# Batch tiles paired with a shift, and every stage placed by a position on one axis

## The chip, the cores and the metric

The kernel runs on one core of a Trainium2 chip. The metric is the device time of one execution in microseconds (us). The core has TensorE (PE) for matmuls, VectorE (DVE), ScalarE (ACT) and GpSimd (POOL); SyncE (SP), ACT and POOL also issue transfers. All data is float32, so each matmul of the program shows as two records in the trace.

## The reference

1024 users are in the batch, each with 50 rows of 300 numbers (`x`) and 200 label rows of 300 numbers. K = 200 labels, E = 300.

```python
mask = sign(sum(abs(x), axis=2))
q1 = attn_pool(x, mask, w1, b1, w2)          # softmax over the 50 rows of exp of a score, then a weighted sum
q2 = attn_pool(x, mask, w3, b3, w4)
h = concatenate([q1, q2], axis=1) @ w5 + b5  # 1024 x 300
f6 = h @ w6 + b6
iu, ju = triu_indices(300, k=1)              # 44850 pairs
g = (v @ v.T)[iu, ju]
cross = h[:, iu] * h[:, ju] * g              # 1024 x 44850
f7 = cross @ w7 + b7                         # w7: 44850 x 300
out8 = concatenate([f6, f7], axis=1) @ w8 + b8
return einsum('bu,bku->bk', out8, label_embedding)
```

## The kernel before

**Tiles and units.** The 1024 users are eight batch tiles of 128. The 44850 pairs are laid out as 351 tiles of 128 pairs (`NT`), grouped in 91 units (`NU`) of mostly four tiles. A unit's left factors are one 128-row tile of h (transposed, pairs on the partitions), its right factors a buffer `sring` that is read back from a copy of h in DRAM (`hrows`); 25 such buffers (`BUFS`) serve the 91 units, three are resident at a time (`SSLOTS`). The last three units ("own") take both factors from such buffers, 26 small transfers for six buffers.

**Main stage.** Two batch tiles form a group (`GB = 2`, `L = 256` columns), and four groups follow one another, 91 units each. For each unit DVE makes the products (`products`, L867: left x right over n x 256 columns into `cring`, four slots, so DVE may be four units ahead of PE). PE multiplies each product tile with its w7 tile (`unit`, L546): n x 2 matmuls of 128 x 128 by 128 x 300 into one PSUM bank for each batch tile. w7 is read once per group: ACT issues a load for every two units (`w7_load`, up to 8 tiles, 1200 KB) two blocks ahead into `wring` (three slots) and multiplies each w7 tile by its factor g (`w7_scale`, L695) two units ahead.

**Pooling.** The batch is 16 halves of 64 users. For one half DVE makes 56 score rows (`score_row`, L795, 128 x 300 each), ACT 28 absolute sums (`absolute`, L627), then come small steps: `exps`, `maxima`, `softexp`, `weights` (L834), 28 narrow matmuls (`pool_rows`, L496), `denominators`, a transpose (`turn`, L484) and, for several halves together, the product with w5 (`mix`, 18 matmuls, L511), which gives h. `features_out` writes it to `hT` and to DRAM. x comes in pieces of 128 x 7 x 300 (1050 KB, L336), four for a half, through nine slots.

**Labels.** `label_row` (L893) multiplies a label row of 128 users with `out8` and sums over 300: 200 rows for each batch tile. SP loads them in chunks of five rows (750 KB, L340) through 13 slots, in the memory that x used. After the main stage four of every five chunks are shared: DVE makes the product of the whole chunk (L889), ACT the five sums (`sums`, L704).

**Order.** Every engine's program is written out over phases: phase -1 is the head (halves 0 to 3, before the first unit), phases 0 to 3 are the four groups, phase 4 is the tail (80 chunks of labels, the last two batch tiles). The other twelve halves all lie in units 0 to 74 of phase 0 (`HALVES`, `X_UNTIL = 75`), the labels of group g in units 11 to 90 of the phase after it. In the head `fold_w8` stands at step 9. Three units before the end of each group `out8_from_f6` puts eight matmuls (four for each batch tile) on PE. All engines run their lists in order.

## Time and profile before

| | |
|---|---|
| runs of the kernel before | 1917.06 us median of 3 (1915.41 to 1917.81) |
| the profiled execution | 1916.95 us, its span 1915.2 us |
| first main matmul (L546) | 169.44 us |
| last main matmul ends | 1759.8 us |
| PE, DVE, ACT busy | 1626.4, 1437.1, 1014.9 us |
| moved | 590.69 MB, mean 308 GB/s |

The span runs from the first to the last instruction of the profiled execution; the execution's time is 1.75 us more. The table cuts it in three: a head up to the first main matmul, the main stage, and a tail of labels. In a row with a start, the first number is the start and the second the duration, both in us.

### The profile page before, as it was taken

The page shows a single profiled execution, that of the slowest core. Times are in us where ns is not written, and L with a number is a line of the kernel's source. Part 1 is how long each engine was busy: PE and PEld are TensorE (multiplying, and loading weights), DVE is VectorE, ACT ScalarE, POOL GpSimd, SP SyncE. Part 2 cuts the span into 40 slices and gives each one's busy share as a digit, 9 for nine tenths or more (in the row PEclk, how much of TensorE's full clock was granted, in tenths as well). Part 3 has the DMA queues.
Part 4 walks back from the last instruction along what each step waited for, and adds up shares of the span by engine and source line. Part 5 has one row for each costly group of instructions (what it writes and reads, how often), then busy time and mean ns, then how long its engine had stood idle before and what let it go on. Part 6 is the DMA issues. An engine that isn't in the chain of part 4 may idle for free.

```text
span 1915.2 us, 24356 instructions
## 1 busy us (share of the span) xinstructions
PE 1626.4 (85%) x7106; PEld 1173.8 (61%) x7106; DVE 1437.1 (75%) x5126; ACT 1014.9 (53%) x3118; POOL 41.3 (2%) x86
## 2 busy tenths in 40 slices
PE   0656899998999999999999999999999999998000
PEld 0334666666667677777776777777677777775000
DVE  8764999899893257778763777787447777874996
ACT  4434677677674344444444444444344444543998
POOL 0001000100100100000000000000000000000000
PEclk9757999999999999999999999999999999999555
DMA  6247567566665979999997899999979999997996
GB/s 271 107 164 263 209 245 291 220 261 260 229 229 202 348 290 357 364 367 368 413 343 268 312 362 361 361 389 407 291 261 364 357 364 357 404 390 221 401 417 247
DMA packets 112003, 590.69 MB, mean 308 GB/s; under 512 B 13940, under 2 KB 29069, under 8 KB 81661
## 3 DMA queue, kind: packets, MB, share of 16 engines
q1 hardware_dynamic: 81373, 368.22, 51.5%
q10 hardware_dynamic: 27680, 217.89, 29.4%
q0 software_dynamic: 2816, 3.01, 0.5%
q8 instruction: 57, 0.93, 0.2%
q14 instruction: 77, 0.63, 0.1%
HBM read 585.28 MB, written 3.79 MB: 308 GB/s over the span
## 4 chain that ended last, share of the span: by engine, by line
PE 67%; DVE 17%; ACT 9%; issue 3%; DMA 3%; POOL 0%; SPq 0%; ACTq 0%; DVEq 0%; POOLq 0%
PE bank L546 60%; DVE junk L795 11%; ACT stream L704 7%; PE bank L511 3%; DVE cring L867 3%; PE bank L496 2%; DMA sring<-hrows 2%; ACT absjunk L627 1%; DVE wts L834 1%; PE bank L559 1%; DMA wring<-in_w7p 1%; PE bank L554 0%; DVE small L824 0%; DVE small L823 0%; PE bank L484 0%
## 5 line engine op out<-in xcount | busy, mean ns | idle before, releaser
L546 PE MATMUL bank<-wring,cring 128*128 128x300 f32 x5616 | 1442.0, 419 | 50.8 <-DVE cring L867 50.0
L546 PEld LDWEIGHTS bank<-wring,cring 128*128 128x128 f32 x5616 | 1067.5, 191 | 417.8 <-DVE cring L867 63.3
L695 ACT ACTIVATE wring<-wring,gcol 128x300 f32<-128x300 f32 x1404 | 636.1, 532 | 674.6 <-DMA wring<-in_w7p 469.7
L893 DVE SCALAR_TENSOR_TENSOR stream<-stream,out 128x300 f32<-128x300 f32 x1280 | 519.5, 464 | 0.0
L867 DVE TENSOR_TENSOR cring<-lefts,sring 128x1024 f32<-128x1024 f32 (+2 forms) x232 | 274.7, 1186 | 178.1 <-PE bank L546 173.7
L795 DVE SCALAR_TENSOR_TENSOR junk<-stream,ubc 128x300 bf16<-128x300 f32 x896 | 356.8, 463 | 0.0
L867 DVE TENSOR_TENSOR cring<-hT,sring 128x1024 f32<-128x1024 f32 (+1 forms) x120 | 144.5, 1206 | 146.3 <-PE bank L546 125.8
L627 ACT ACTIVATE absjunk<-stream 128x300 bf16<-128x300 f32 x448 | 195.6, 439 | 0.5
L704 ACT ACTIVATE stream<-stream 128x300 f32<-128x300 f32 x320 | 139.4, 449 | 0.0
L496 PE MATMUL bank<-stream,wts 128*32 128x300 f32 x896 | 68.2, 461 | 52.4 <-DVE small L837 52.4
L889 DVE TENSOR_TENSOR stream<-stream,out 128x1500 f32<-128x1500 f32 x64 | 105.8, 1712 | 4.9 <-ACT out L614 4.9
L893 DVE DVE_READ_ACCUMULATOR stream<-stream,out 128x1 f32 x1280 | 103.5, 81 | 0.0
L627 ACT ACTIVATION_READ_ACCUMULATOR absjunk<-stream 128x1 f32 x448 | 84.6, 189 | 0.0
L496 PEld LDWEIGHTS bank<-stream,wts 128*32 128x32 f32 x896 | 30.6, 120 | 87.6 <-issue 62.4
L795 DVE DVE_READ_ACCUMULATOR junk<-stream,ubc 128x1 f32 x896 | 71.6, 80 | 0.0
L867 DVE TENSOR_TENSOR cring<-sring 128x1024 f32<-128x1024 f32 (+1 forms) x12 | 11.5, 955 | 72.4 <-issue 43.5
L511 PE MATMUL bank<-poolT,w5sb 128*128 128x64 f32 (+7 forms) x252 | 62.3, 392 | 4.0 <-ACT poolT L614 4.0
L704 ACT ACTIVATION_READ_ACCUMULATOR stream<-stream 128x1 f32 x320 | 63.7, 199 | 0.0
L511 PEld LDWEIGHTS bank<-poolT,w5sb 128*128 128x128 f32 (+3 forms) x252 | 41.9, 217 | 24.8 <-issue 12.2
L617 ACT ACTIVATE hT<-bank,bcol 128x64 f32<-128x64 f32 (+3 forms) x21 | 8.0, 381 | 66.2 <-PE bank L511 66.2
L834 DVE TENSOR_TENSOR wts<-small,onehot 128x896 f32<-128x896 f32 x16 | 17.4, 1086 | 23.5 <-ACT small L640 23.5
L484 PE MATMUL bank<-ident,flat 128*128 128x128 f32 (+1 forms) x72 | 13.1, 303 | 25.7 <-ACT flat L644 24.9
(59 smaller groups left out, 220.8 us busy)
## 6 DMA issues: line engine op xcount, KB each, us to landing
stream<-in_label SPq DMA_DIRECT2D x320, 750.0 KB, 8.7
wring<-in_w7p ACTq DMA_DIRECT2D x164, 1200.0 KB, 8.5
stream<-in_x SPq DMA_DIRECT2D x64, 1050.0 KB, 9.4
sring<-hrows SPq DMA_DIRECT2D x76, 512.0 KB
wring<-in_w7p ACTq DMA_DIRECT2D x8, 1050.0 KB, 7.7
wring<-in_w7p ACTq DMA_DIRECT2D x8, 600.0 KB, 6.7
sring<-hrows SPq DMA_DIRECT2D x16, 176.0 KB
lefts<-hrows SPq DMA_DIRECT2D x20, 128.0 KB, 3.3
```

What stands on the lines that cost most here:

```text
L496: pe.matmul(dst[j * M:(j + 1) * M, 0:E], wts[:, j * T + t].rearrange("p h b -> p (h b)"), xring[:, (s * XCH + c) % XSLOTS, t - CHUNK[c][1] ...
L511: mm = pe.matmul(dst[0:n, 0:nb], w5sb[0:nk, q, o:o + n], poolT[0:nk, q % NCH, q // NCH, b0:b0 + nb], start=(q == 0), stop=(q == 2 * NCH - 1))
L546: mm = pe.matmul(acc[(g * GB + b) % 4][:, 0:E], lhs, w, start=(t == 0), stop=(t == NT - 1))
L559: mm = pe.matmul(dst[:, 0:E], f7T[0:n, b, c, :], w8sb[0:n, NCH + c, :], start=False, stop=(c == NCH - 1))
L627: nc.scalar.activation(absjunk[:, k % 2, :], xring[:, n % XSLOTS, t - CHUNK[c][1], :], ACT.Abs, accum_out=absum[:, s % 3, at:at + 1]).then ...
L695: ins = nc.scalar.activation(w, w, ACT.Copy, scale=gcol[:, t:t + 1])
L704: ins = nc.scalar.activation(row, row, ACT.Copy, accum_out=score[:, m % GB, q0 + k:q0 + k + 1])
L795: ins = nc.vector.scalar_tensor_tensor(out=junk[:, k % 2, r % 2, :], in0=xring[:, n % XSLOTS, t - CHUNK[c][1], :], scalar=1.0, in1=ubc[:, ...
L834: nc.vector.tensor_tensor(wts[:], prob[k].rearrange("p h t -> p t h").unsqueeze(3).to_broadcast([P, TT, 2, UB]), onehot[:].unsqueeze(1).un ...
L867: nc.vector.tensor_tensor(cut(cring[:, k % CSLOTS]), in0, cut(sring[:, nb % SSLOTS]), ALU.mult).then_inc(c_ready, 1)
L889: nc.vector.tensor_tensor(rows, rows, out8[:, m % (2 * GB), :].unsqueeze(1).to_broadcast([P, LR, E]), ALU.mult).then_inc(l_product, 1)
L893: ins = nc.vector.scalar_tensor_tensor(out=row_in, in0=row_in, scalar=1.0, in1=out8[:, m % (2 * GB), :], op0=ALU.mult, op1=ALU.mult, accum ...
```

## The change

The phases go; every stage has a position on one axis instead, from -34 (`START`) to 473. Positions 0 to 406 (`POS = 407`) are units of the main stage; unit p uses the unit table at p mod 91.

- **Pairs with a shift.** Even batch tiles begin at positions 0, 91, 182, 273, odd ones at 43, 134, 225, 316 (`SHIFT = 43`), each for 91 positions; an odd tile begins in the middle of the table and wraps around. So positions 0 to 42 have one batch tile, 43 to 363 two, 364 to 406 one. In numbers of the table: 167 tiles with one matmul each, 1237 with two, 167 with one; 2808 matmuls in all, as before.
- **Single units.** Where one batch tile is live, DVE makes the products with one `scalar_tensor_tensor` of 128 columns for each tile, which takes in the factor g, and w7 isn't scaled by ACT; PE waits for the w7 load itself. Where two are live, product and scaling are as before, with 4-dimensional operands.
- **w7** is streamed in rounds of 91 positions: 206 blocks, where it was 184.
- **h in DRAM** is kept for each batch tile by itself (`hrows[b]`, rows of 128 numbers, where they were 256), so a buffer of two live tiles is two loads. Left tiles lie in `lefts` for four batch tiles. POOL stores repeated rows with fewer transfers (`again`).
- **Pooling** of the halves goes by the list `DOTS`: halves 0 and 1 in positions -34 to -21, half 2 in -20 to -7, half 3 in -6 to 5, halves 4 and 5 to 42, 6 to 9 in 43 to 88, and 10 to 15 in stretches of 14 positions every 23, to 228. `mix` follows for each batch tile (seven of the eight behind position 0). From half 10 on x has four slots, one half.
- **Labels** begin at position 102 (`LATER = 11` behind a tile's end). Batch tiles 0 to 5 have theirs over the 43 or 48 positions that follow, at half the rate inside `DOTS`; 65 rows of tile 6 lie in 375 to 406. 67 chunks are left for the tail, where there were 80. The label ring has 7 slots until x is done and 13 then.
- **out8** is made for each batch tile in one piece (`out8_all`) four positions behind its end; `out8_from_f6` ahead of the group's end is gone.
- `fold_w8` and `folded_out` stand at -23 (step 11), and the first two w7 loads behind them.

```diff
-    GB = 2
-    G = NBT // GB
-    L = GB * P
+    SHIFT = next(k for k, u in enumerate(UNITS) if u[1] == 6)
+    BEGIN = [NU * (b // 2) + SHIFT * (b % 2) for b in range(NBT)]
+    END = [p + NU for p in BEGIN]
+    POS = END[-1]
...
+    DOTS = [(-34, -27), (-27, -20), (-20, -6), (-6, 6), (6, 24), (24, 43), (43, 54), (54, 65), (65, 77), (77, 89),
+            (100, 114), (123, 137), (146, 160), (169, 183), (192, 206), (215, 229)]
...
+    WIDE = 10
+    X_SLOT = [n % XSLOTS if n < WIDE * PARTS else XSLOTS - PARTS + n % PARTS for n in range(NS * PARTS)]
...
+    EXP, MAX, SOFT, WEIGH, POOL, DEN, POOL_OUT, TURN, MIX = range(9)
+    LATE = (0, 1, 1, 2, 3, 8, 8, 9, 12)
+    HEAD = {0: (0, 2, 3, 3, 3, 6, 7, 7, 0), 1: (0, 1, 1, 2, 2, 6, 6, 6, 7)}
+    X_FREE = 7
...
+    NARROW = LSLOTS - 6
...
             def s_load(n):
-                g, buf = n // BUFS, n % BUFS
...
+                for b in live_at(n):
+                    tiles = sring[:, n % SSLOTS, b % 2]
...
+                    if buf < OWN:
...
+                        sp.dma_start(tiles.rearrange("p j l -> p (j l)"), src).then_inc(s, 16)
+                        continue
...
+            for q in range(START, STOP):
+                for n in [n for n in range(XSLOTS, NS * PARTS) if DOTS[X_BEFORE[n] // PARTS][1] + X_FREE == q]:
+                    x_load(n)
...
+            def unit(p):
...
+                pe.wait_ge(c_ready, p + 1)
+                if SHIFT <= p < SHIFT + BOTH:
+                    pe.wait_ge(w7_ready, p - SHIFT + 1)
+                else:
+                    pe.wait_ge(w7_in[n_block % WSLOTS], 16 * (n_block // WSLOTS + 1))
...
+                    for b in live(p):
+                        mm = pe.matmul(acc[b % 4][:, 0:E], cring[0:rows, p % CSLOTS, b % 2, j0 + j, :], w,
+                                       start=(p == BEGIN[b] and j == 0), stop=(p == END[b] - 1 and j == n - 1))
...
+            def products(p):
...
+                if len(tiles) == 1:
+
+                    b = tiles[0]
+                    for j in range(j0, j0 + n):
...
+                        ins = nc.vector.scalar_tensor_tensor(
+                            out=cring[0:rows, p % CSLOTS, b % 2, j, :], in0=one, scalar=gcol[0:rows, t:t + 1],
+                            in1=sring[0:rows, nb % SSLOTS, b % 2, j, :], op0=ALU.mult, op1=ALU.mult)
+                    ins.then_inc(c_ready, 1)
+                    return
...
```

## Rows read from the trace of the kernel before

**Rows 1.** The page: busy time of each engine, and TensorE's clock in 40 slices.

```profile
PE 1626.4 (85%) x7106; PEld 1173.8 (61%) x7106; DVE 1437.1 (75%) x5126; ACT 1014.9 (53%) x3118; POOL 41.3 (2%) x86
...
PEclk9757999999999999999999999999999999999555
```

**Rows 2.** Windows: stretch, length, busy us (records) of PE, PEld, DVE, ACT, POOL, PEclk, DMA share, GB/s.

```profile
170.00:300.00 130.00, 116.16 (x588) 80.83 (x587) 128.07 (x556) 96.33 (x341) 0.00 (x0) 0.98 0.66 246
800.00:990.00 190.00, 190.00 (x754) 142.94 (x753) 151.62 (x532) 84.11 (x187) 0.56 (x1) 1.00 0.98 378
990.00:1034.00 44.00, 41.46 (x154) 28.83 (x153) 17.59 (x50) 13.47 (x30) 0.55 (x1) 0.96 0.87 280
1766.00:1915.00 149.00, 0.00 (x0) 0.00 (x0) 134.24 (x224) 139.59 (x641) 1.08 (x2) 0.51 0.86 347
```

**Rows 3.** Groups by line and shape: busy us, mean ns | idle before, releasers.

```profile
L546 PE MATMUL bank<-wring,cring 128*128 128x300 f32 x5600 | 1437.4, 419 | 50.8 <-DVE cring L867 50.0 <-ACT wring L695 0.6
...
L893 DVE SCALAR_TENSOR_TENSOR stream<-stream,out 128x300 f32<-128x300 f32 x1280 | 519.5, 464 | 0.0
L795 DVE SCALAR_TENSOR_TENSOR junk<-stream,ubc 128x300 bf16<-128x300 f32 x896 | 356.8, 463 | 0.0
...
L867 DVE TENSOR_TENSOR cring<-lefts,sring 128x256 f32<-128x256 f32 x8 | 3.4, 425 | 16.0 <-PE bank L546 11.6 <-DMA lefts<-hrows 4.4
```

**Rows 4.** Timeline of DVE in phase 0: start, duration, instruction.

```profile
186.07 1.22 DVE L867 TENSOR_TENSOR cring<-lefts,sring 128x1024 f32<-128x1024 f32 x1
187.21 0.46 DVE L795 SCALAR_TENSOR_TENSOR junk<-stream,ubc 128x300 bf16<-128x300 f32 x1
...
187.60 0.46 DVE L795 SCALAR_TENSOR_TENSOR junk<-stream,ubc 128x300 bf16<-128x300 f32 x1
...
204.72 0.17 DVE L814 TENSOR_SCALAR masked<-absum 128x28 f32<-128x28 f32 x1
...
206.96 1.22 DVE L867 TENSOR_TENSOR cring<-hT,sring 128x1024 f32<-128x1024 f32 x1
```

**Rows 5.** Chain of waits in the head, 33 to 90 us: start, duration, what.

```profile
47.33 6.47 PE bank L496 x54
...
61.76 0.41 ACT brow L614
...
72.21 8.63 PE bank L511 x36
```

**Rows 6.** Timeline of PE at the first main matmul.

```profile
169.44 10.13 PE L546 MATMUL bank<-wring,cring 128*128 128x300 f32 x32 [12.61 <-DVE cring L867]
```

**Rows 7.** Transfers issued from 300 to 430 us: count, KB each, median us to landing.

```profile
wring<-in_w7p ACTq DMA_DIRECT2D x12, 1200.0 KB, 5.7
```

**Rows 8.** Transfers issued from 800 to 990 us.

```profile
stream<-in_label SPq DMA_DIRECT2D x49, 750.0 KB, 8.1
wring<-in_w7p ACTq DMA_DIRECT2D x22, 1200.0 KB, 8.8
```

**Rows 9.** Chain of waits, the whole span: PE's side work.

```profile
312.74 3.66 PE bank L496 x54
...
498.91 9.66 PE bank L511 x36
...
1041.59 3.62 PE bank L559 x12
```

**Rows 10.** Timeline of all engines at the end of phase 1.

```profile
1001.02 1.22 DVE L867 TENSOR_TENSOR cring<-sring 128x1024 f32<-128x1024 f32 x1 [7.38 <-DMA sring<-hrows]
...
1002.27 1.14 SPq L382 DMA_DIRECT2D sring<-hrows  x3
...
1017.03 1.22 DVE L867 TENSOR_TENSOR cring<-sring 128x1024 f32<-128x1024 f32 x1 [12.83 <-issue]
...
1018.31 15.48 PE L546 MATMUL bank<-wring,cring 128*128 128x300 f32 x52 [2.54 <-DVE cring L867]
```

**Rows 11.** Timeline of PE at the last main matmuls.

```profile
1754.30 5.51 PE L546 MATMUL bank<-wring,cring 128*128 128x300 f32 x20
```

More of the change, by code:

```diff
@@ L139, in rec_kernel @@
     LSLOTS = 13
+    ROUNDS = [1 << k for k in range(FOLD.bit_length() - 1)]
     SSLOTS = 3
@@ new lines, in rec_kernel @@
+    LATER = 11
+    EARLY_ROWS = 65
+    LABELS_BY = {START - 1: 0}
+    for q in range(START, POS):
+        done = 0
+        for b in range(NBT - 1):
+            steps = range(END[b] + LATER, END[b + 1] + LATER if b < NBT - 2 else POS)
+            share = [1 if any(a <= k < z for a, z in DOTS) else 2 for k in steps]
+            rows = K if b < NBT - 2 else EARLY_ROWS
+            done += rows * sum(w for k, w in zip(steps, share) if k <= q) // sum(share)
+        LABELS_BY[q] = done
+    TAIL_CHUNKS = (NBT * K - LABELS_BY[POS - 1]) // LR
@@ L152, in rec_kernel, with labels_by, released @@
+    def labels_by(q):
+        return LABELS_BY[min(q, STOP - 1)]
+    def released(n):
+        return (l_summed if SHARED[n] else l_used), sum(SHARED[k] == SHARED[n] for k in range(n + 1))
     ctx = ExitStack()
```

687 lines of the change are left out of this document (328 added, 359 removed).

## The prediction

> **What bounds the kernel now.** I read the busy shares first. PE is busy 85% of the span and DVE 75%, so neither binds throughout, and the last three slices have PE's clock at half: that is the tail, which has no matmuls [rows 1]. So the span is read in three parts, and each part has its own limit.
>
> The head lasts 169.4 us until the first main matmul, which came after DVE's first product [rows 6]. Four halves are pooled one behind another there.
>
> The main stage lasts 1590.4 us, to 1754.30 + 5.51 = 1759.8 [rows 11]. In its steady phases PE is busy 190 of 190 us, 754 records, 0.252 us each, so 0.504 us for one matmul of the program [rows 2]; 2808 of them are 1415 us. PE stood 50.8 us ahead of these matmuls, nearly all for DVE's products [rows 3]. DMA is at a share of 0.98 and 378 GB/s in the same window, so I take 385 GB/s as the most that this mix of transfers gets. In phase 0 it is DVE that is full: 128.07 of 130 us, PE 116.16 [rows 2]. There a position costs nine score rows at 187.60 - 187.21 = 0.39 us and a product of 1.14 us (186.07 to 187.21), 4.66 in all [rows 4], against eight matmuls, 4.03. A half adds 2.24 us of small steps (204.72 to 206.96) and about 1.5 for weights and denominators. Over 75 positions and twelve halves DVE needs some 395 us, PE 350 to 360.
>
> The tail lasts 1915.2 - 1759.8 = 155.4 us. ACT is busy 139.59 of 149 there, DVE 134.24 [rows 2]: 64 shared chunks on ACT, 2.18 us each; what is left, 9.6 us behind ACT's last sum, is the last store and the end.
>
> **Part 1, the head: 169.4 becomes 110.** Two halves instead of four must be pooled for the first product, but 196 score rows stand ahead of it in DVE's list. These are 77 us from about 12. ACT is held by `folded_out` until 61.76 + 0.41 [rows 5], as before; then eight absolute sums at 0.44, and `maxima` of half 1 starts near 67, weights end near 72, `pool_rows` at the low clock takes up to 6.5 us [rows 5], the mix of tile 0 ends near 90 (8 to 9 us [rows 5]). ACT waits for this mix and then has 14 absolute sums of half 2, to 97; DVE's `maxima` of half 2 waits for them, and about 19 score rows and the weights follow: the first single product near 109.5. The loads of h end before (first A store near 88, left tiles by 106). I take 110, bounds 104 and 118.
>
> **Part 2, positions 0 to 42, one tile: 116.** PE: 167 matmuls x 0.504 = 84, two `pool_rows` at 3.66 [rows 9], three transposes, one mix of 128 columns, a slow start of the clock: 102. DVE: 140 score rows (55 us), small steps 8, and 167 products of 128 columns. This instruction isn't in the trace. From below, 128 columns at the pace of a 1024-column product (1.14 for 1024) are 0.14; from above, a 256-column product lasts 0.425 [rows 3] and half of its columns are 0.13 less, 0.29. Score and label rows of 300 columns last 0.46 [rows 3] and issue every 0.39; the 1024-column product less the 256-column one is 0.80 us for 768 columns, 0.13 for 128, and 0.07 of its 1.14 is left over for the start: 0.20. I take 0.20: 33 us, DVE 96, bounds 88 and 111. DMA: w7 is needed at full rate for half the work, 25 MB, and twelve x pieces fall in here (13 MB), h 2.7 MB: 41 MB, 106 us at 385 GB/s. It doesn't come evenly. A w7 block is 4.03 us of PE work here (1.23 MB, 305 GB/s). It landed in 5.7 us where SP's queue had gaps [rows 7] and in 8.8 where labels filled it [rows 8]. 1.23 MB at 385 GB/s are 3.2 us, which leaves 2.5 for the way; 8.8 less 2.5 is 195 GB/s, half. So while four x pieces drain, w7 gets 190 GB/s, 6.4 us for a block, and 22 us of this lose 8 us each time. Three bursts, the first while three blocks are resident, PE's side work covering some: 14 us on top of 102. Bounds 102 and 130.
>
> **Part 3, positions 43 to 363, two tiles: 1409.** PE: 2474 matmuls, 1247 us; eleven `pool_rows` 40; transposes 5; six mixes, whose group form took 9.66 [rows 9], taken at 6.5, 39; six `out8_all` and transposes at 5 (half of [rows 9]'s 3.62, and four matmuls of f6 more), 30: 1361. Short dips of the clock add 5: one is in the window of 990 to 1034, 0.96 [rows 2]. DVE: 347 us of products, 560 score rows, 1154 label rows, eleven times small steps, some 1060: hidden in sum, and in the densest stretch (positions 100 to 236: 936 rows, 147 us of products, 22 us of steps, 536 of PE's 597) too. Phase 0's loss goes away, since its score rows are spread over 229 positions.
>
> Two waits take a part back. First, the own units. Buffer 22 can load only behind product 88. Before, it was issued at 1002.27 and product 89 came at 1017.03; PE stood 2.54 us [rows 10], with the 5.3 us of `out8_from_f6` in between. That cover is gone, and the buffer is six transfers on SP's queue and not three, buffer 23 ten and not five, with rows half as long. So 8 + 4 us where labels share the queue; three such places in here and at 364, less where the queue is less full: 25 (bounds 5 and 45). Second, SP's queue in positions 100 to 236. The stretch moves 91 MB of labels, 21 of x, 82 of w7 and 19 of h, 213 MB in 597 us, 357 GB/s of 385. x has one half's slots, so the four pieces are issued two positions (8 us) before the first is read, behind label loads. DVE would stand about 12 us for each of six halves; it is up to four units, 16 us, ahead of PE, and has about 10 us to spare in each 23 positions. I take 3 us a half, 18 (bounds 0 and 70). Sum 1361 + 5 + 25 + 18.
>
> One rule of the Trainium skill bears on the rate. Its page "DMA: Bandwidth & Descriptors", section Bandwidth, gives about 358 GB/s as what one core gets from HBM; the window at 378 GB/s [rows 2] is above it, so the measurement stands. By 358 the two single stretches would be 114 and 119 us.
>
> **Part 4, positions 364 to 406, one tile: 113.** PE has 84 + 5, DVE 43 + 33. DMA has 23 MB of w7, 23 label chunks (17.7 MB) and 2 MB of h: 42.7 MB, 111 us. In the first eleven positions labels come at 4.2 rows a position, and w7 gets its half: 35 us where PE needs 22. The rest, 28 MB, is 73 us. With some start 113; bounds 92 and 130.
>
> **Part 5, the tail: 129.** 67 chunks, 53 shared: 53 x 2.18 = 115.6 us on ACT, DVE 115. Three to four us for tile 7's f7 and out8, then the 9.6 as before. Labels of tile 6 are there at once, so the 4 us start on `out` goes. Bounds 125 and 134.
>
> **Sum:** 110 + 116 + 1409 + 113 + 129 = 1877 us of span, plus 1.75: **1879 us**, against 1916.95 of the same profiled execution and 1917.06 of the median. Against before: head -59, main stage +48, tail -26. 0.2% (3.8 us) is about what a measurement of this kernel can tell.
>
> **Rivals.**
> - *A, the likeliest (0.50):* as above; its own range is 1850 to 1910.
> - *B, PE bounds it all (0.23):* w7 is favoured or buffered enough in the single stretches, and the own loads hide. Then 106 + 103 + 1375 + 94 + 127 + 2 = 1807, up to 1850. For it: DMA at 0.98 and PE at 190 of 190 in one window [rows 2]. Against it: there PE asked for 152 GB/s of w7, not 305.
> - *C, SP's queue starves DVE, slower (0.17):* the 12 us of waiting for x in each of six halves come through whole, because a wait of DVE also delays its products and its lead isn't won back in the score stretch (4.3 us a position on DVE, 4.03 on PE). Then 54 us more than in A, 1933. It decides from 34 us more, 6 us a half. For it: 357 of 385 GB/s, one queue in order. Against: 16 us of lead.
> - *D, the clock falls in the single stretches (0.05):* gaps in PE's work at w7 waits could drop it to 1.2 GHz, a matmul to 1.01 us. Each single stretch that ran so throughout would last 169 + side work, 60 us more: 1939 for one. Against it: 0.98 with PE at 116 of 130 us [rows 2]. For it: the clock's low level in the head, where PE is busy in pieces [rows 1]. The Trainium skill, "TensorE: Matmul & The Clock Gate", section HAM oscillation, tells of such a kernel, whose waits for DMA brought the clock down in every round; this rule is what D is.
> - *E, gains and losses cancel (0.05):* 1913 to 1921.
>
> **Chances.** A gives 0.49 faster and 0.01 same; B 0.23 faster; C 0.14 slower, 0.02 same, 0.01 faster; D 0.04 slower, 0.01 faster; E 0.02 same, 0.02 slower, 0.01 faster. Together: faster 0.75, same 0.05, slower 0.20. The range for 8 in 10 cuts off the lower half of B and the upper half of C and D: 1825 to 1932.
>
> **What the profile will show.** First main matmul at 104 to 118. In positions 0 to 42 and 364 to 406 PE idle until w7 lands, DMA share over 0.95 and w7 landing in 8 us or more; B if PE is over 95% busy there. DVE's label and score rows waiting for `in_x` and `in_label` in 500 to 900 us: a few us a half for A, over 10 for C. Single products 0.20 us apart. PE waiting for `cring` some 10 us at positions 89 to 91 of each round. The clock's line below 9 in the single stretches would be D. The prediction is wrong if label loads keep w7 out longer than half, or if a wait of ACT in its new order (a mix, x) holds back the scaling of w7, which I costed at nothing because it is two units ahead.

## The result, and the profile after

The changed kernel takes 1860.16 us (median of 4 runs, 1856.23 to 1862.87); the kernel before took 1916.93 (4 runs). The ratio is 0.9709, with a 95% interval of 0.9695 to 0.9724: faster by 2.9%. The forecast was 1879 us, in a range of 1825 to 1932, so the time is 19 us under it and inside case A's own range. The profiled execution took 1859.29 us, its span is 1857.5.

The first main matmul of a position cuts the span in stages:

| stage (positions) | forecast, us | after, us | before, us |
|---|---|---|---|
| head | 110 | 106.7 | 169.4 |
| 0 to 42, one tile | 116 | 118.8 | |
| 43 to 363, two tiles | 1409 | 1397.6 | |
| 364 to 406, one tile | 113 | 105.1 | |
| main stage together | 1638 | 1621.5 | 1590.4 |
| tail | 129 | 129.2 | 155.4 |
| span | 1877 | 1857.5 | 1915.2 |

So the head gives 62.7 us, the tail 26, and the main stage takes back 31. The page of the kernel after, to be held against [rows 1]: busy times, and TensorE's clock.

```profile
PE 1615.5 (87%) x7142; PEld 1165.1 (63%) x7142; DVE 1479.9 (80%) x5516; ACT 919.1 (49%) x2844; POOL 33.4 (2%) x62
...
PEclk9889999999999999998999999999999999999655
```

PE is busy 11 us less than before in a span that is 58 shorter. The windows of the four stages behind the head, columns as in [rows 2]:

```profile
106.70:225.50 118.80, 102.88 (x507) 71.42 (x508) 108.17 (x500) 38.12 (x157) 3.52 (x6) 1.00 0.87 340
225.50:1623.10 1397.60, 1373.77 (x6004) 1008.01 (x6002) 1074.40 (x3973) 708.89 (x1918) 23.95 (x41) 0.99 0.89 332
1623.10:1728.20 105.10, 93.98 (x351) 64.23 (x351) 95.11 (x400) 1.71 (x5) 0.54 (x1) 1.00 1.01 418
1728.20:1857.50 129.30, 9.13 (x18) 4.12 (x17) 109.75 (x181) 117.15 (x535) 1.08 (x2) 0.51 0.81 326
```

In both single stretches PE has idle time: 15.9 us in the first, 11.1 in the second. The second has the DMA engines at a share of 1.01; the first has DVE busy 108 of 119. With two tiles PE is busy 98% of the time. What PE waited for in the first, by the view of waits (us in total, times, longest; 2.1 us of the first line lie ahead of the first main matmul):

```profile
PE bank L600 <- DVE cring L905: 10.9, 10, 2.2
...
PE bank L600 <- DMA wring<-in_w7p: 7.1, 5, 2.1
```

In the second it is 8.6 us for w7 and 2.9 for products. The groups that answer to [rows 3], and two more (L905 is the product of a single unit, L917 that of a pair, L935 the label row, L819 the score row):

```profile
L600 PE MATMUL bank<-wring,cring 128*128 128x300 f32 (+1 forms) x5616 | 1448.0, 419 | 52.8 <-DVE cring L917 19.6
...
L935 DVE SCALAR_TENSOR_TENSOR stream<-stream,out 128x300 f32<-128x300 f32 x1335 | 546.4, 466 | 0.9 <-DMA stream<-in_label 0.2
L917 DVE TENSOR_TENSOR cring<-lefts,sring 128x1024 f32<-128x1024 f32 (+2 forms) x309 | 368.3, 1193 | 205.1 <-PE bank L600 202.6
L819 DVE SCALAR_TENSOR_TENSOR junk<-stream,ubc 128x300 bf16<-128x300 f32 x896 | 364.2, 466 | 4.3 <-DMA stream<-in_x 4.2
...
L905 DVE SCALAR_TENSOR_TENSOR cring<-lefts,gcol,sring 128x128 f32<-128x128 f32 x334 | 95.2, 348 | 16.8 <-PE bank L600 15.7
...
L917 DVE TENSOR_TENSOR cring<-sring 128x1024 f32<-128x1024 f32 (+1 forms) x12 | 11.5, 956 | 72.4 <-DMA sring<-hrows 49.1
```

Three readings come from here. Score rows waited 4.2 us for x in all, label rows 0.2 for labels: SP's queue starved nobody. The products of the own units (the last group, twelve of them) waited 72 us on DVE, most of it for `sring`; this is a wait of DVE, of which PE sees what is left when its four units of lead are used up. And PE's idle time ahead of the main matmuls is 52.8 us where it was 50.8 [rows 3]. But 12.6 of the 50.8 lay ahead of the very first main matmul [rows 6], in the head, and only 2.1 of the 52.8 do. Inside the main stage PE's idle time has grown, and it lies elsewhere: 15.7 us of it are waits for w7 itself, 19.6 are waits for products of pairs, nearly all at the own units.

### The profile page after: what moved, and what is told of

It is laid out like the page before. It is cut to its first block, busy times and chain, and to the rows that moved or that the text cites. A ratio compares the mean times of both kernels' runs of the same rounds, so it can differ in the third digit from the quotient of the medians.

```text
span 1857.5 us, 25035 instructions
## 1 busy us (share of the span) xinstructions
PE 1615.5 (87%) x7142; PEld 1165.1 (63%) x7142; DVE 1479.9 (80%) x5516; ACT 919.1 (49%) x2844; POOL 33.4 (2%) x62
## 3 DMA queue, kind: packets, MB, share of 16 engines
q1 hardware_dynamic: 105157, 368.23, 52.8%
## 4 chain that ended last, share of the span: by engine, by line
PE 72%; DMA 7%; ACT 7%; DVE 7%; SPq 4%; issue 2%; ACTq 0%; POOL 0%; DVEq 0%; POOLq 0%
PE bank L600 64%; ACT stream L747 6%; DMA wring<-in_w7p 5%; DVE junk L819 3%; PE bank L549 3%; SPq L438 3%; PE bank L563 2%; DMA sring<-hrows 2%; DVE stream L935 1%; PE bank L612 1%; PE bank L610 1%; DVE cring L917 1%; DVE cring L905 1%; ACT absjunk L663 1%; SPq L444 0%
## 5 line engine op out<-in xcount | busy, mean ns | idle before, releaser
L600 PE MATMUL bank<-wring,cring 128*128 128x300 f32 (+1 forms) x5616 | 1448.0, 419 | 52.8 <-DVE cring L917 19.6
L600 PEld LDWEIGHTS bank<-wring,cring 128*128 128x128 f32 (+1 forms) x5616 | 1064.1, 191 | 420.8 <-DVE cring L905 30.4
L738 ACT ACTIVATE wring<-wring,gcol 128x300 f32<-128x300 f32 x1237 | 565.1, 533 | 608.8 <-PE bank L600 340.3
L935 DVE SCALAR_TENSOR_TENSOR stream<-stream,out 128x300 f32<-128x300 f32 x1335 | 546.4, 466 | 0.9 <-DMA stream<-in_label 0.2
L917 DVE TENSOR_TENSOR cring<-lefts,sring 128x1024 f32<-128x1024 f32 (+2 forms) x309 | 368.3, 1193 | 205.1 <-PE bank L600 202.6
L819 DVE SCALAR_TENSOR_TENSOR junk<-stream,ubc 128x300 bf16<-128x300 f32 x896 | 364.2, 466 | 4.3 <-DMA stream<-in_x 4.2
L747 ACT ACTIVATE stream<-stream 128x300 f32<-128x300 f32 x265 | 115.5, 441 | 0.1
L935 DVE DVE_READ_ACCUMULATOR stream<-stream,out 128x1 f32 x1335 | 109.9, 82 | 0.0
L905 DVE SCALAR_TENSOR_TENSOR cring<-lefts,gcol,sring 128x128 f32<-128x128 f32 x334 | 95.2, 348 | 16.8 <-PE bank L600 15.7
L931 DVE TENSOR_TENSOR stream<-stream,out 128x1500 f32<-128x1500 f32 x53 | 89.6, 1717 | 3.5 <-DMA stream<-in_label 1.8
L819 DVE DVE_READ_ACCUMULATOR junk<-stream,ubc 128x1 f32 x896 | 74.0, 83 | 0.0
L917 DVE TENSOR_TENSOR cring<-sring 128x1024 f32<-128x1024 f32 (+1 forms) x12 | 11.5, 956 | 72.4 <-DMA sring<-hrows 49.1
L747 ACT ACTIVATION_READ_ACCUMULATOR stream<-stream 128x1 f32 x265 | 50.5, 190 | 0.0
L563 PE MATMUL bank<-poolT,w5sb 128*128 128x128 f32 (+3 forms) x288 | 48.2, 297 | 1.0 <-ACT poolT L652 0.8
L563 PEld LDWEIGHTS bank<-poolT,w5sb 128*128 128x128 f32 (+3 forms) x288 | 35.2, 164 | 14.4 <-issue 4.5
L655 ACT ACTIVATE lefts<-bank,bcol 128x128 f32<-128x128 f32 x16 | 5.9, 366 | 43.6 <-PE bank L563 42.7
## 6 DMA issues: line engine op xcount, KB each, us to landing
stream<-in_x SPq DMA_DIRECT2D x64, 1050.0 KB, 12.6
```

The lines of the kernel that those rows point to most:

```text
L563: mm = pe.matmul(dst[0:n, 0:P], w5sb[0:nk, q, o:o + n], poolT[0:nk, q % NCH, q // NCH, :], start=(q == 0), stop=(q == 2 * NCH - 1))
L600: mm = pe.matmul(acc[b % 4][:, 0:E], cring[0:rows, p % CSLOTS, b % 2, j0 + j, :], w, start=(p == BEGIN[b] and j == 0), stop=(p == END[b] - ...
L738: ins = nc.scalar.activation(w, w, ACT.Copy, scale=gcol[:, t:t + 1])
L747: ins = nc.scalar.activation(row, row, ACT.Copy, accum_out=score[:, m % 2, q0 + k:q0 + k + 1])
L819: ins = nc.vector.scalar_tensor_tensor(out=junk[:, k % 2, r % 2, :], in0=xring[:, X_SLOT[n], t, :], scalar=1.0, in1=ubc[:, hd, 0:E], op0=A ...
L905: ins = nc.vector.scalar_tensor_tensor(out=cring[0:rows, p % CSLOTS, b % 2, j, :], in0=one, scalar=gcol[0:rows, t:t + 1], in1=sring[0:rows ...
```

## The experiments

Each kernel is the changed one with the edit shown. Stage times are read as in the table above.

**Half of w7 in the single stretches.** Each block of positions 0 to 42 and 364 to 406 loads its first half alone and uses it twice, which leaves out half of those blocks' w7.

```diff
+                z = a + half(n) * E
                 act.dma_start(wring[:, n % WSLOTS, 0:z - a], w7p[:, a:z]).then_inc(w7_in[n % WSLOTS], 16)
```

> The changed kernel, but in positions 0 to 41 and 364 to 406 each w7 block loads only half of its tiles (the second half of the tiles is multiplied with the first half's weights, so half of w7 is left out there). If DMA bounds the single stretches (my theory): the first goes from 118.8 us to 104 to 108, the second from 105.1 to 92 to 95, the run 20 to 25 us shorter. If DVE bounds them (busy 108 of 118.8 and 95 of 105.1 us): no more than 3 us each.

Measured: 1840.27 us, ratio 0.9606 (0.9586 to 0.9626). The first stretch took 112.5 us (-6.3), the second 94.0 (-11.1), the rest is within 2 us. So the forecast of this experiment held in the second stretch and was too high in the first (104 to 108 were expected). The windows of both stretches:

```profile
106.80:219.30 112.50, 102.35 (x507) 71.59 (x508) 107.76 (x499) 38.66 (x159) 3.52 (x6) 1.00 0.72 261
1619.10:1713.00 93.90, 91.80 (x352) 65.86 (x351) 92.58 (x395) 2.00 (x7) 0.54 (x1) 0.98 0.92 335
```

With DMA no longer full, PE is busy 91.80 of 93.90 us in the second: transfers were its bound. In the first PE still idles 10 us, and DVE is busy 107.76 of 112.50.

**One wide product in the single stretches.** The factor g is left out there, so that DVE makes one product of all tiles of a unit.

```diff
-                    for j in range(j0, j0 + n):
...
-                        ins = nc.vector.scalar_tensor_tensor(
...
+                    nc.vector.tensor_tensor(cring[0:rows, p % CSLOTS, b % 2, j0:j0 + n, :],
+                                            left_of(left, b)[0:rows].unsqueeze(1).to_broadcast([rows, n, P]),
```

> The changed kernel, but where one batch tile is live the product of a unit is one tensor_tensor over all its tiles without the factor g (g is left out there). It should last 0.6 us where four single ones take 1.05, 19 us less of DVE in each single stretch. If DVE bounds them: 118.8 us becomes 105 to 109 and 105.1 becomes 95 to 98, the run 15 to 22 us shorter. If DMA bounds them: no more than 3 us each.

Measured: 1853.11 us, ratio 0.9674 (0.9658 to 0.9690). The first stretch took 115.0 us (-3.8), the second 105.2, unchanged. The interval lies just beside that of the changed kernel. **Both edits together**:

> e1_half_w7 and e2_wide together (half of w7 and the factor g left out in the single stretches). Alone they took 6.3 and 3.8 us off the first single stretch of 118.8 us. If DMA and DVE take turns there, and the one hides what the other frees: 102 to 107. If something else holds it (PE's side work, ACT): 108 to 112.

One run, 1828.85 us. The first stretch took 107.6 us (-11.2, against 6.3 and 3.8 alone), the second 91.2 (-13.9). With one run of it, a difference of 1 us isn't read. So the first stretch is held by transfers and by DVE in turns, the second by transfers, with DVE next behind them.

**w7 scaled by ACT in the last stretch.** This puts the factor g back to ACT from position 43 on, so DVE makes wide products in the last stretch and the result is the full one.

```diff
-                if SHIFT <= p < SHIFT + BOTH:
+                if SHIFT <= p:
...
-                    if SHIFT <= q + AHEAD < SHIFT + BOTH:
+                    if SHIFT <= q + AHEAD < POS:
```

> The changed kernel, but in positions 364 to 406 ACT, which is idle there (1.7 of 105 us busy), scales w7 two units ahead as in the paired stretch, and DVE makes one product for a unit. DVE has 19 us less. If DMA bounds this stretch: 105.1 us stays or becomes up to 110, since w7 is wanted two units earlier. If DVE's products do: 95 to 98.

Measured: 1871.19 us, ratio 0.9766 (0.9740 to 0.9792), slower than the changed kernel. The last stretch took 117.5 us, 12.4 more. DVE had been no bound there. The waits of this kernel say what took its place: ACT waited 36.2 us for w7 loads in the stretch, and PE 11.7 us for ACT's scaling. A w7 block is needed two units earlier, and the transfers were full already. About half of the 12.4 us is TensorE's clock: in the window of 1623 to 1740 us its mean is 0.94, PE is busy 99.8 us where it was 94.0 in the changed kernel, and from 1636 to 1644 the granted clock is 0.50 with PE at work, after a stretch of 8 us in which PE was busy 4.8.

**Plain loads for the own units.** Every own buffer is loaded like any other, as one transfer of 128 rows of 2 KB for each tile; the pairs of these units are then wrong ones.

```diff
-                    if buf < OWN:
+                    if buf < BUFS:
...
-                return len(live_at(n)) * (1 if buf < OWN else (5, 5, 3, 3, 5, 5)[buf - OWN])
+                return len(live_at(n)) * 1
```

> The changed kernel, but the six buffers of the own units are each loaded by one plain transfer for a batch tile, where they take 26 (the pairs of these units are wrong, their number of bytes is higher). If the number of transfers on SP's queue is what delays them: PE's gaps at positions 89 to 91 (0.8, 10, 2.7, 3.7 us by round) go below 2 us and positions 176 to 186 from 61.2 us to 40 to 45, the run 12 to 25 us shorter. If it is the label loads queued ahead of them: within 5 us of the changed kernel.

Measured: 1838.09 us, ratio 0.9603 (0.9581 to 0.9624). The pair stretch took 1375.5 us, 22.1 less, the others within 2.3 us of the changed kernel. The own units come four times; the time of the positions around each, in us, with the kernels of the next three experiments:

| positions | changed | plain loads | issued by ACT | in one transfer | left once |
|---|---|---|---|---|---|
| 85 to 94 | 45.6 | 41.9 | 45.5 | 41.9 | 42.4 |
| 176 to 185 | 61.2 | 49.0 | 50.1 | 59.0 | 58.3 |
| 267 to 276 | 40.4 | 39.7 | 51.9 | 50.0 | 39.0 |
| 358 to 369 | 44.5 | 38.3 | 48.7 | 48.0 | 40.8 |

Each column is one profiled execution. How far such a number can be trusted is told by the kernels whose own loads are the changed kernel's (half of w7, wide product, both, scaled by ACT, and `fold_w8` first, further down): they have 43.3 to 45.7 us at the first place, 59.3 to 61.8 at the second, 40.2 to 46.2 at the third and 40.3 to 48.7 at the fourth, which runs into the last stretch, where most of them differ. So a difference of a few us at one place says little, and the 40.4 of the changed kernel at the third is on the low side. Their pair stretches took 1392.0 to 1401.6 us.

Here is the second of these places in the changed kernel, all engines (L438, L444 and L446 are the small transfers on SP's queue):

```profile
828.01 1.23 DVE L917 TENSOR_TENSOR cring<-sring 128x1024 f32<-128x1024 f32 x1 [9.41 <-DMA sring<-hrows]
...
829.26 7.32 SPq L438 DMA_DIRECT2D sring<-hrows  x6
...
836.75 1.29 SPq L444 DMA_DIRECT2D sring<-hrows  x4
...
840.20 0.29 SPq L446 DMA_DIRECT2D sring<-hrows  x1
...
842.04 1.23 DVE L917 TENSOR_TENSOR cring<-sring 128x1024 f32<-128x1024 f32 x1 [10.07 <-issue]
```

And PE there:

```profile
843.32 7.43 PE L600 MATMUL bank<-wring,cring 128*128 128x300 f32 x20 [8.60 <-DVE cring L917]
```

Product 88 waits 9.4 us for its buffers, and only when it is done may SP load the last buffer of product 89 (number 22), six transfers that take 7.3 us to issue; product 89 comes 14 us after product 88, and PE stands 8.6 us.

The first of the four places is the comparison that matters most. The transfers are the same, six for buffer 22 among them, but no label is loaded yet:

```profile
428.40 1.23 DVE L917 TENSOR_TENSOR cring<-sring 128x1024 f32<-128x1024 f32 x1 [8.69 <-DMA sring<-hrows]
...
434.16 1.22 DVE L917 TENSOR_TENSOR cring<-sring 128x1024 f32<-128x1024 f32 x1 [2.57 <-issue]
```

Product 89 comes 5.8 us after product 88 there. In the three later rounds, with label loads in SP's queue, it comes 14.0, 13.2 and 17.2 us after it. With plain loads the four distances are 6.6, 6.7, 8.1 and 7.3 us. So small transfers are not late by themselves; they are late in the rounds that load labels, and there plain ones hardly are. The windows of 820 to 860 us, the changed kernel:

```profile
820.00:860.00 40.00, 29.47 (x107) 20.89 (x106) 19.66 (x87) 14.32 (x45) 0.00 (x0) 0.87 0.77 233
```

and with plain loads:

```profile
820.00:860.00 40.00, 36.01 (x159) 24.96 (x161) 32.22 (x134) 20.98 (x60) 0.00 (x0) 0.91 0.93 350
```

While the small transfers run, all transfers together bring 233 GB/s with the engines at a share of 0.77; with plain ones they bring 350 at 0.93. Three further kernels vary how the small transfers are issued.

**The own loads issued by ACT** instead of SP. ACT issues a load three places earlier in its list than SP did, behind a wait for the same product of DVE.

```diff
+                    if t == q + 3 and n + SSLOTS in BUFFERS and (n + SSLOTS) % BUFS >= OWN:
+                        act.wait_ge(c_ready, t + 1)
+                        loads[0](n + SSLOTS, act)
```

> The changed kernel with the loads of the own units' six buffers issued by ACT (which waits for DVE's product three positions ahead of its own place) and not by SP. Theory (they wait in SP's list and behind its label loads): PE's gaps at positions 88 to 91 (10 and 3.7 us in the second and fourth round) go below 3 us, positions 176 to 186 from 61.2 us to 45 to 52, the run 8 to 20 us shorter. Rival (the transfers themselves, their number and half-length rows, are the time, in whatever queue; or ACT, held by its wait, is late with the scaling of w7): within 5 us of the changed kernel, or slower.

Measured: 1875.32 us, ratio 0.9785 (0.9759 to 0.9812), 15 us slower than the changed kernel. The second place took 50.1 us for 61.2, inside what was expected of it: product 89 comes 8.4 us after product 88 there, not 14.0, with the same six transfers.

```profile
832.39 1.22 DVE L926 TENSOR_TENSOR cring<-sring 128x1024 f32<-128x1024 f32 x1 [10.49 <-issue]
...
840.75 1.23 DVE L926 TENSOR_TENSOR cring<-sring 128x1024 f32<-128x1024 f32 x1 [4.39 <-issue]
```

The gap of 8.6 us is gone, but PE has new ones, of 6.6 us at this place, 4.7 at the third, and 5.3 and 3.6 at the fourth. All but the last end with ACT's scaling of w7: ACT is late for it, since its own list stands while it waits for DVE and issues. The waits of this kernel in the pair stretch, two rows of them (what waited, for what: us in total, times, longest):

```profile
ACT wring L742 <- issue: 47.6, 8, 7.2
...
PE bank L604 <- ACT wring L742: 20.8, 12, 6.6
```

**Both tiles' rows in one transfer** where the shape allows it. The rows of all tiles lie in one tensor; the number of issues falls, bytes and row length stay. The ordinary buffers become one transfer for both tiles too. The transfers over 44, 44 and 40 partitions stay one for each tile, so buffer 22, for which product 89 waits, has six transfers as before.

```diff
-        hrows = [nc.dram_tensor(f"hrows{b}", [A_ROWS + B_ROWS + C_ROWS + D_ROWS, P], F32, kind="Internal").ap()
-                 for b in range(NBT)]
+        hall = nc.dram_tensor("hall", [NBT * RB, P], F32, kind="Internal").ap()
...
+                    src = bass.AP(hall.tensor, (BASE[b0] + row) * P, [[rpitch, r1 - r0], [step, nt], [1, P]])
+                    sp.dma_start(dst, src).then_inc(s, 16)
```

> The changed kernel with the DRAM copies of h in one tensor, so that a buffer of two live batch tiles is one transfer (the own units' six buffers 38 a round and not 52, buffers 23 and 24 five each and not ten). The bytes and the lengths of rows are unchanged. Theory (the number of transfers that SP must issue): PE's gaps at positions 88 to 91 shrink, positions 176 to 186 from 61.2 us to 50 to 56, the run 6 to 15 us shorter. Rival (e3_own_plain gained by other things: longer rows, no spread over few partitions): within 3 us of the changed kernel.

Measured: 1869.63 us, ratio 0.9771 (0.9742 to 0.9800), slower than the changed kernel. PE's longest gaps at the last three places are 10.1, 7.8 and 8.4 us where they were 8.6, 1.5 and 3.7. Since buffer 22 is loaded as before (product 89 comes 14.4 us after product 88 at the second place), this kernel doesn't tell whether fewer issues for it would help; its loss lies elsewhere and isn't traced. The window shows that merging the others didn't make the transfers faster as a whole:

```profile
820.00:860.00 40.00, 29.26 (x104) 20.08 (x102) 21.42 (x95) 14.26 (x44) 0.00 (x0) 0.87 0.82 247
```

**Left buffers of the own units loaded once over 128 rows.** Their three transfers of 44, 44 and 40 rows read the same repeated rows, so one transfer of 128 brings the same data.

```diff
-                        for k, (r0, r1) in enumerate(((0, REST), (REST, 2 * REST), (2 * REST, P))):
+                        for k, (r0, r1) in enumerate(((0, P),) if left else ((0, REST), (REST, 2 * REST), (2 * REST, P))):
```

> The changed kernel with the left factors of the first two own units (buffers 20 and 22) read in one transfer over 128 partitions for each batch tile, not three over 44, 44 and 40 (the repeated rows in DRAM hold the same numbers, so the result is the same): 44 transfers a round and not 52, and buffer 22, which can only be asked for behind product 88, is two transfers and not six. Theory (a transfer over few partitions in short rows is slow on DMA, and buffer 22 is the one that DVE stands for): product 89 comes 3 to 6 us earlier behind product 88 in positions 88 to 91, positions 176 to 186 from 61.2 us to 52 to 57, the run 5 to 12 us shorter than the changed kernel, the fastest version so far. Rival (as in e9_merged, the buffers behind it hold DVE just as long): within 4 us of the changed kernel.

Measured: 1847.51 us (6 runs, 1845.52 to 1852.04), ratio 0.9637 (0.9609 to 0.9664). This is the fastest version that computes the whole reference; its interval doesn't meet that of the changed kernel, and it is some 0.7% under it. The pair stretch is 1384.7 us, 12.9 less, and under all those of 1392.0 to 1401.6. The same place in this kernel:

```profile
822.48 1.22 DVE L917 TENSOR_TENSOR cring<-sring 128x1024 f32<-128x1024 f32 x1 [7.45 <-DMA sring<-hrows]
...
823.73 1.97 SPq L438 DMA_DIRECT2D sring<-hrows  x2
...
835.67 1.22 DVE L917 TENSOR_TENSOR cring<-sring 128x1024 f32<-128x1024 f32 x1 [9.22 <-issue]
...
836.94 7.43 PE L600 MATMUL bank<-wring,cring 128*128 128x300 f32 x20 [5.79 <-DVE cring L917]
```

Two transfers are issued in 1.97 us where six took 7.32, and yet product 89 comes 13.2 us after product 88 and not 14.0. So the time of issuing is not what it waits for; the landing is. Bytes and row length are those of the changed kernel, so the gain comes with fewer and wider transfers alone. The 12.9 us come in pieces of 1 to 4 at the four places, each too small to be told from the spread above; only their sum can.

What holds the landing stays open between two causes. In both kernels SP issued a label load of 750 KB shortly ahead of buffer 22 (at 826.78, 2.5 us ahead, in the changed kernel), and the first round, which has none, is quick. And a w7 load on ACT's queue was under way: from 836 to 838 us it brought 0.45 MB while all of SP's queue brought 0.04; in the first round w7 loads were issued at 424.5 and 433.0 us, and none between the two products. No run takes one of them away and leaves the rest.

**No shift.** `SHIFT = 0`: tiles run in pairs as before, all stages by positions, halves 0 to 3 in the head, the other twelve in positions 0 to 228; labels over the 91 positions behind a pair.

```diff
-    SHIFT = next(k for k, u in enumerate(UNITS) if u[1] == 6)
+    SHIFT = 0
...
-    DOTS = [(-34, -27), (-27, -20), (-20, -6), (-6, 6), (6, 24), (24, 43), (43, 54), (54, 65), (65, 77), (77, 89),
+    DOTS = [(-36, -29), (-29, -22), (-22, -15), (-15, -8), (0, 17), (17, 34), (34, 51), (51, 67), (67, 78), (78, 89),
```

> The changed kernel with SHIFT = 0: two batch tiles begin together as before the change, four halves are pooled in the head, 364 positions, 80 chunks of labels in the tail; score rows spread over the positions, storage of h by batch tile and all else as in the changed kernel (out8 of the odd tile six positions later). If the shift is what gains: head 150 to 160 us, main stage 1550 to 1575, tail 152 to 158, 1870 to 1895 in all, 10 to 35 us slower than the changed kernel. If the spreading of the score rows is the gain and the shift only pays its own costs: 1865 or less.

Measured: 1917.50 us (10 runs), ratio 0.9996 (0.9983 to 1.0010): no difference from the kernel before, and slower than either expectation. The head took 153.1 us, the four rounds 395.4, 410.7, 418.3 and 373.5, the tail 166.2. The tail is long because labels were held back four positions and the odd tile's `out8` six, which this edit needed. Windows of the four rounds, first the kernel before:

```profile
169.40:654.70 485.30, 452.88 (x2332) 311.64 (x2332) 405.11 (x1689) 325.07 (x1110) 27.09 (x54) 0.99 0.66 243
654.70:1025.40 370.70, 367.28 (x1439) 272.32 (x1438) 263.17 (x890) 160.88 (x362) 1.11 (x2) 1.00 0.94 353
1025.40:1394.60 369.20, 366.55 (x1439) 272.55 (x1438) 263.55 (x892) 160.91 (x362) 1.08 (x2) 1.00 0.93 349
1394.60:1759.80 365.20, 365.14 (x1439) 271.49 (x1438) 261.95 (x890) 158.88 (x357) 0.68 (x2) 1.00 0.93 348
```

and this one:

```profile
153.10:548.50 395.40, 390.62 (x1811) 287.50 (x1811) 256.64 (x887) 239.10 (x722) 7.02 (x12) 0.99 0.62 223
548.50:959.20 410.70, 398.45 (x1778) 291.40 (x1779) 332.06 (x1272) 215.70 (x612) 7.61 (x13) 0.98 0.88 333
959.20:1377.50 418.30, 400.53 (x1711) 291.69 (x1711) 320.20 (x1199) 192.46 (x500) 8.11 (x14) 0.97 0.89 340
1377.50:1751.00 373.50, 368.52 (x1438) 272.96 (x1438) 284.53 (x1004) 158.06 (x355) 1.63 (x3) 0.99 0.96 364
```

The first round gives 90 us and the other three take 97. PE's busy time moved (1551.9 us before, 1558.1 here). Its idle time was 32.4 us in the first round and 6.1 in the rest; here it is 4.8 and 35.0. These are two effects and not one. Spreading the score rows took 27.6 us of idle time out of the first round. What is new in the others lies mostly at the own units, where PE's longest gaps are 9.5, 9.6 and 4.1 us; before, none there was over 2.7. They come with h stored for each tile, twice as many small transfers of half the row length, and with the cover of `out8_from_f6` gone. No run has the spreading with the old storage.

**Labels of tile 6 early.** 110 of its rows instead of 65 lie ahead of the tail, and those of tile 5 end at its neighbour's end.

```diff
-            steps = range(END[b] + LATER, END[b + 1] + LATER if b < NBT - 2 else POS)
+            steps = range(END[b] + LATER, END[b + 1] + LATER if b < NBT - 3 else END[b + 1] if b < NBT - 2 else POS)
...
-    EARLY_ROWS = 65
+    EARLY_ROWS = 110
```

> The changed kernel with the labels of batch tile 5 finished by position 363 (37 positions and not 48), and 110 rows of tile 6 in positions 375 to 406, not 65: 58 chunks in the tail and not 67. The same number of rows lies in the last single stretch. Theory (positions 327 to 363 have room on DVE, DMA at most full; the tail costs 1.86 us a chunk): tail 129.2 to 112 to 114, single stretch 105.1 +-3, positions 273 to 363 up to 4 us longer, the run 12 to 18 us shorter. Rival (DMA is full in both places and what is moved is paid there): the run within 5 us of the changed kernel.

Measured: 1856.10 us, ratio 0.9689 (0.9664 to 0.9713); the difference from the changed kernel is within the intervals. The tail took 116.2 us (-13.0), positions 273 to 363 382.3 (+11.5). So the rival held. 8 of the 11.5 us are at positions 358 to 369, which took 52.5. The labels fill the transfers ahead of the last own units. Window of 1480 to 1590 us, the changed kernel:

```profile
1480.00:1590.00 110.00, 110.00 (x438) 82.75 (x437) 80.69 (x268) 48.61 (x108) 0.00 (x0) 1.00 0.97 359
```

and with the labels early:

```profile
1480.00:1590.00 110.00, 109.60 (x435) 82.22 (x434) 92.54 (x334) 48.62 (x109) 0.00 (x0) 1.00 1.01 397
```

PE's gap behind it, ahead of a product of the last own units:

```profile
1625.33 7.44 PE L600 MATMUL bank<-wring,cring 128*128 128x300 f32 x20 [10.72 <-DVE cring L917]
```

**This and the own loads on ACT together:**

> e5_own_on_act and e6_labels_early together. If they lie at different places their gains add: 20 to 35 us shorter than the changed kernel, 1825 to 1840 us. If both only shift the same DMA time: less than 12 us shorter.

Measured: 1865.01 us, ratio 0.9734 (0.9710 to 0.9757), between the two; the gains don't add. The 10.7 us gap is gone, and PE has gaps of 4.6, 5.4 and 6.8 us at the second, third and fourth place instead, each ended by ACT's scaling.

**`fold_w8` first in the head.** `W68 = -27` where it was -23.

> The changed kernel with fold_w8, folded_out and the first two w7 loads at position -27 and not -23, ahead of the first pool_rows. Theory (ACT stands for the folded product until 61 us, which makes maxima of half 1 wait until 66): ACT stands until about 44 instead, maxima of half 1 comes at 60 to 62, the first main matmul at 101 to 104 instead of 106.7, the run 3 to 6 us shorter. Rival (w8 and w6 land too late, or the softmax of half 0 is held in turn): first main matmul at 106 or later.

Measured: 1864.69 us (6 runs, 1857.45 to 1875.82), ratio 0.9738 (0.9709 to 0.9766): no gain, so the rival held. In the profiled run, at the top of that spread, the head took 117.2 us; what it took in the others isn't known. Its chain and a window; L573 is the first step of `fold_w8`, L563 the mix:

```profile
36.55 10.54 PE bank L573 x18
...
85.48 10.77 PE bank L563 x36
```

```profile
85.50:96.30 10.80, 10.74 (x36) 7.35 (x36) 10.80 (x55) 0.76 (x3) 0.00 (x0) 0.50 0.92 382
```

The changed kernel's chain in the head, for comparison, and with [rows 5]:

```profile
47.33 5.97 PE bank L549 x54
53.35 5.58 PE bank L573 x18
...
79.69 6.12 PE bank L563 x36
```

Behind `pool_rows` the same 18 matmuls took 5.58 us, as the first work of PE after 28.6 us of standing 10.54. That is twice the time, as at half the clock, but the profile can't confirm it: its first entry for the clock is at 61.6 us in this kernel (at 51.9 in the changed one), and a granted clock of 1.00 in a window ahead of it says nothing. The mix ran at a granted clock of 0.50 here, the 1.2 GHz level, and took 10.77 us; in the changed kernel it took 6.12, at 1.00:

```profile
79.70:85.80 6.10, 6.10 (x36) 4.32 (x36) 6.10 (x31) 0.74 (x2) 0.00 (x0) 1.00 1.00 420
```

## Why the prediction held, point by point

**Head, 110 forecast, 106.7.** The chain is the one forecast: ACT is free at 61.6, eight absolute sums, weights, `pool_rows`, mix, then ACT's sums of half 2 and the first single product. The term that was too large is the mix, 8 to 9 us taken from [rows 5]; it took 6.12, since that row had been measured at the low clock (0.50 from 72.2 to 80.9 us) and this mix ran at the full one.

**Positions 0 to 42, 116 forecast, 118.8.** PE's 102 us are right (102.88). The single product is mis-sized: 0.20 us were taken, and four of them take 1.05, by the starts of the product and of the row behind it:

```profile
1680.77 1.14 DVE L905 SCALAR_TENSOR_TENSOR cring<-lefts,gcol,sring 128x128 f32<-128x128 f32 x4 [0.79 <-PE bank L600]
1681.82 0.46 DVE L935 SCALAR_TENSOR_TENSOR stream<-stream,out 128x300 f32<-128x300 f32 x1
```

That is 0.26 each, near the upper bound of 0.29, and 44 us for 167 of them instead of 33. DVE has 108 us in the stretch instead of 96 and is a limit beside the transfers. The 14 us of waiting for w7 came as 7.1 for w7 and 8.8 for products; the runs above share them out (6.3 and 3.8, together 11.2). So the total is near by luck in part: waiting for DVE's products stands where half of the waiting for w7 had been put. The sign for this stretch, a DMA share over 0.95, didn't come (0.87).

**Positions 43 to 363, 1409 forecast, 1397.6.** The work of PE was costed at 1361; it is 1247 for the main matmuls and 108 for side work (eleven `pool_rows` at 3.66, mixes at 5.84 for the 6.5 taken, `out8_all` at 4.52), 1355. PE idled 23.4 us, most of it at the own units (25 forecast). The clock was at its low level for 24 us in four pieces (at 444, 837, 864 and 1615 us), some 16 of them with PE at work, so it cost some 8 (5 forecast). Some 11 us more of PE's busy time are not attributed. **The term that failed is the 18 us of SP's queue:** it was nothing, since score rows waited 4.2 us in all. The stretch of 357 GB/s was thought near a limit of 385; the limit is higher (below), and DVE's lead may have taken in the rest. Case C, at 1933, needed 12 us for each of six halves; these 4.2 us are what all halves had together.

The own units were forecast at 25 us over three places, and PE stood 19.6 us for products of pairs. The condition, "where labels share the queue", is right: product 89 is 5.8 us behind product 88 without labels and 13 to 17 with them. But the gap of 8 + 4 us came at one place alone (8.6, then 1.5 at the third and 3.7 at the fourth), and the working by the number of issues isn't borne out: with two transfers issued in place of six the product is nearly as late (13.2 for 14.0 us). On ACT's queue it is 8.4 us behind, with the scaling of w7 paying for it. Plain loads give 22 us back. The runs show that these small transfers (44, 40, 7 or 22 partitions, rows of 512 bytes) land late beside label loads. Fewer and wider transfers with the same rows give 12.9 us of the 22; whether the rest is due to longer rows isn't settled, since the plain loads change both.

**Positions 364 to 406, 113 forecast, 105.1.** The mechanism was right: transfers at 1.01, PE waiting 8.6 us for w7, and half of w7 gives 11.1 us back. The rate is mis-sized: 385 GB/s were taken and 418 came; 42.7 MB are 111 us by the one and 102 by the other. The landing of w7 was forecast at 8 us or more in the single stretches; the medians are 8.1 us in the first (issued from 130 to 220 us) and 9.9 in this one (1630 to 1720):

```profile
wring<-in_w7p ACTq DMA_DIRECT2D x17, 1200.0 KB, 8.1
...
wring<-in_w7p ACTq DMA_DIRECT2D x18, 1200.0 KB, 9.9
```

**Tail, 129 forecast, 129.2.** The steps are the forecast ones, and two small errors cancel: ACT's last sum ends 121.6 us into the tail (119 forecast), and 7.7 us are left behind it (9.6 forecast).

**The main stage as a whole** costs 31.1 us more than before: PE's busy time is 18.7 us more (1570.6 for 1551.9), mostly since seven mixes at about 5.84 instead of three at 9.66 (12) and the pooling of one half more (3.7) lie in it now, and its idle time 12.4 more (50.9 for 38.5). This is the price of the head and the tail. The pooling is of one half and not two, since half 2 is still pooled in the head, at 98.6 us. And the prediction read the 50.8 us of [rows 3] as idle time of the main stage, where 12.6 of them lie ahead of it.

**How much was luck.** The stages were off by -3, +3, -11, -8 and 0 us, so the total of 19 us is no sum of large errors that cancel. Within the stages they do cancel in part: the two limits of the first single stretch, and in the pair stretch 18 us of SP's queue too much against 11 that aren't attributed.

**The rivals.** B (PE bounds it all, 1807 to 1850) fell by the single stretches: only with half of w7 and no factor g did they come to 107.6 and 91.2. C fell as told. D fell too: the clock is 1.00 in both single stretches in spite of PE's waits, of 2.2 us at the longest. It isn't far away, though: with w7 scaled by ACT the clock fell in the last stretch, as told above. In the changed kernel it dropped at the own units. Two windows at the second of them:

```profile
838.00:844.00 6.00, 0.68 (x2) 0.52 (x3) 1.96 (x6) 2.28 (x7) 0.00 (x0) 0.50 0.30 88
846.00:848.00 2.00, 2.00 (x7) 1.49 (x6) 0.02 (x2) 0.00 (x0) 0.00 (x0) 0.69 0.12 25
```

TensorE stood from 834.7 to 843.3; the clock fell in the gap and was back at 848, with PE at work for 4.7 us. By the time that PE worked at half the clock, the four dips cost some 1.5 to 3 us each. The Trainium skill ("TensorE: Matmul & The Clock Gate", section HAM oscillation) tells of a kernel whose waits for DMA bring the clock down each time; its waits are longer than those of the single stretches here, so this trace doesn't contradict it.

**What made the gain.** The kernel with no shift has nearly every other part of the change and gains nothing. Its head is 16 us shorter than before; which part of the new lists does that isn't traced. The shift's head is 46 us shorter still, since the first product needs two pooled halves and not four (a third is pooled ahead of it by the order of the lists). The tail is 37 us shorter than without the shift, 26 shorter than before; the difference of 11 is what the edit of that kernel costs itself. Labels of tile 6 are read while tile 7 is still in the main stage. What the shift costs is w7 traffic, 244 MB for 218, and two stretches in which each w7 tile serves one matmul.

## What to carry to other kernels

A stage that can't overlap with anything (a head that fills, a tail that drains) is worth shortening by staggering two streams, if the price is paid where another engine has room. Spreading the score rows took 27.6 us of PE's idle time out of the first round here, and small transfers that came with the rest of the change put as much back in the others: look at each place, not at the sum. Load a buffer over all 128 partitions in one transfer even when that reads repeated rows; it gave 12.9 us here. Small transfers cost most where large ones stand in the same queue, so compare a place that has none. Price an instruction by its own width from a row of the same kind, and a rate by the best window of long rows and not by a mixed one.

## What was not expected of the hardware

- In the last single stretch the transfers brought 418 GB/s over 105 us, at a share of 1.01. The kernel before had 378 in its fullest window [rows 2]. The Trainium skill, "DMA: Bandwidth & Descriptors", section Bandwidth, gives about 358 GB/s as one core's limit, which the prediction quotes, but also says that its table, with 425 GB/s for 16 MB, is of a core whose neighbour is idle, and that each of two gets about 358 when both stream. This kernel runs on one core, and its windows of 378, 397 and 418 are all above 358 and below 425.
- From 820 to 860 us the DMA engines showed a share of 0.77 to 0.82 while they brought 233 to 247 GB/s, where long rows bring 359 at 0.97: worked out from these windows, that is about 300 GB/s for a full share with small transfers among the long ones, where long rows have 370 and up.
- Four chained products of 128 columns, each with a factor for each partition, take 0.26 us apiece, where a row of 300 columns with a sum takes 0.39 by its starts [rows 4].
- Eighteen matmuls took 5.58 us behind other work and 10.54 as the first work of TensorE after 28.6 us of standing; ahead of 51.9 us neither profile has an entry for the granted clock.
- The same small transfers let a product come 5.8 us after the one before it with no label loads in the queue, and 13 to 17 us with them.
